# An adaLN, two-way Mamba and FFN kernel: places of side jobs inside its rounds moved by a table

## What is computed

```
h = layernorm(x) * (1 + ca) + sa                       # ca, sa, ga, ...: rows made from a condition vector
for the backward and the forward direction:            # own weights each
    xi, z = split(h @ in_proj.T)                       # 512 channels each
    xi    = silu(causal_conv4(xi) + conv_b)
    dt, B, C = split(xi @ x_proj.T, [64, 80])
    dt    = softplus(dt @ dt_w.T + dt_b)
    state[t] = exp(dt*A) * state[t-1] + (dt*xi)*B[t]   # 16 states for every channel
    y     = sum_s(state * C) + xi*D ;  y = y * silu(z) ; y = sigmoid(y @ out_proj.T)
x = x + ga * (layernorm(0.5*(yf + yb))*g + b + h)
x = x + gb * ffn(layernorm(x) * (1 + cb) + sb)         # four ternary matmuls, silu and gelu
```

## Time and profile before

| | |
|---|---|
| median of 3 runs | 4754.95 us (4752.24 to 4763.35) |
| span of the profiled execution | 4760.7 us |
| DVE busy | 3894.2 us, 82% |
| PE busy | 4479.5 us, 94% |
| POOL busy | 3320.9 us, 70% |
| ACT busy | 3109.7 us, 65% |
| rounds 1 to 30 | 182.6 to 3318.5 us, 101 to 110 us each |

### The profile page before, as it was taken

One profiled execution on the slowest core, in us unless ns is written; L12 is line 12 of the kernel. 1 busy time (PEld: TensorE's weight loads), 2 busy tenths in 40 slices (PEclk: granted clock), 3 DMA queues, 4 the chain that ended last, 5 costly groups with the idle time before them and its releaser, 6 DMA issues. The chain is left out here.

```text
span 4760.7 us, 67108 instructions
## 1 busy us (share of the span) xinstructions
PE 4479.5 (94%) x24932; PEld 3395.1 (71%) x24932; DVE 3894.2 (82%) x4126; ACT 3109.7 (65%) x5158; POOL 3320.9 (70%) x1559
## 2 busy tenths in 40 slices
PE   7999999999999989999999999998799999999999
PEld 3666666666666666667666667666688888888888
DVE  5999999999999999999999999999854444444452
ACT  6777777777777777777777777777444444444443
POOL 4999999999999999999999999999820000000000
PEclk9999999999999999999999999999999999999999
DMA  7544444444444444444444444444231111010100
GB/s 271 178 142 141 134 151 132 136 134 134 143 139 134 155 132 138 129 139 139 131 147 140 129 130 136 143 142 156 103 123 32 36 32 36 32 36 32 36 23 10
DMA packets 297736, 545.76 MB, mean 115 GB/s; under 512 B 101888, under 2 KB 186624, under 8 KB 262784
## 3 DMA queue, kind: packets, MB, share of 16 engines
q1 hardware_dynamic: 296512, 529.91, 35.6%
q10 hardware_dynamic: 896, 11.54, 0.7%
HBM read 502.77 MB, written 50.14 MB: 116 GB/s over the span
## 5 line engine op out<-in xcount | busy, mean ns | idle before, releaser
L1400 DVE TENSOR_TENSOR_SCAN m_h<-bank,m_state,m_dBx 128x512 f32<-128x512 f32 x1512 | 1841.2, 1265 | 35.0 <-ACT bank L1145 27.2
L868 PEld LDWEIGHTS bank<-ident,m_h 128*128 128x128 f32 x8192 | 980.9, 143 | 417.2 <-issue 345.8
L868 PE MATMUL bank<-ident,m_h 128*128 128x128 f32 x8192 | 1197.6, 276 | 12.9 <-DVE m_h L1408 12.8
L1283 POOL TENSOR_TENSOR m_dBx<-u,m_Bs 128x1024 f32<-128x1024 f32 x432 | 1016.4, 2377 | 0.4 <-DMA m_Bs<-b_dram 0.2
L1283 POOL TENSOR_TENSOR m_dBx<-m_u,m_Bs 128x1024 f32<-128x1024 f32 x432 | 1015.5, 2371 | 1.2 <-DMA m_Bs<-b_dram 1.0
L1294 POOL TENSOR_TENSOR m_h<-m_h,m_Cs 128x1024 f32<-128x1024 f32 x384 | 909.4, 2368 | 105.8 <-ACT m_state L1077 105.1
L1408 DVE TENSOR_TENSOR m_h<-m_h,bank 128x1024 f32<-128x1024 f32 x640 | 767.0, 1198 | 51.7 <-PE bank L850 51.4
L1145 ACT ACTIVATE bank<-m_dt,cols 128x512 f32<-128x512 f32 x864 | 584.8, 688 | 225.2 <-DVE m_h L1400 223.7
L1145 ACT ACTIVATE bank<-dt,cols 128x512 f32<-128x512 f32 x864 | 584.1, 688 | 193.6 <-DVE m_h L1400 191.6
L302 POOL TENSOR_TENSOR mvj<-mvj,norm_c 128x4 f32<-128x4 f32 x16 | 16.5, 1032 | 969.0 <-DVE mvj L263 969.0
L731 PE MATMUL bank<-hT,w_in 128*128 128x512 f32 x1024 | 547.4, 630 | 113.1 <-ACT hT L998 105.8
(11 more groups left out here) (177 smaller groups left out, 5847.1 us busy)
## 6 DMA issues: line engine op xcount, KB each, us to landing
m_Bs<-b_dram SPq DMA_DIRECT2D x256, 1024.0 KB, 6.3
m_Cs<-c_dram SPq DMA_DIRECT2D x384, 256.0 KB, 3.7
m_dg<-d_dram SPq DMA_DIRECT2D x160, 256.0 KB, 3.9
xx<-in_x SPq DMA_DIRECT2D x16, 512.0 KB, 4.9
xn_dram<-xx SPq DMA_DIRECT2D x16, 512.0 KB, 4.5
yb_dram<-m_ysb SPq DMA_DIRECT2D x16, 512.0 KB, 5.0
xx<-xn_dram SPq DMA_DIRECT2D x16, 512.0 KB, 3.8
x_dram<-m_ysb SPq DMA_DIRECT2D x16, 512.0 KB, 5.0
```

The costliest lines, as they stand in the source:

```text
L868: mm = pe.matmul(YB[b][:, o:o + P], h[:, k % NH, m, tok:tok + P], ident[:, :], start=(s == 0 and o == 0), stop=False, is_transpose=True, s ...
L1283: pool.tensor_tensor(dBx[:, dbx_ring(ch, k) % NDBX, :, :], u[ch.batch][:, m, :], Bs[:, k // BP % 2, k % BP, :].unsqueeze(1).broadcast_to(( ...
L1400: dve.tensor_tensor_scan(o, decays, share, initial, ALU.mult, ALU.add).then_inc(S["scan"], 1)
```

## The change

Only places change, no operation. The table `AT`, the banks of three jobs, and these constants are new; SP's loads are listed in another order; `job` and `row_job` count the rows of the last round at their new places among the jobs of their bank.

```diff
-AT = {J_LN: (0, 2), J_X: (1, 3, 9, 10), J_CONV: (13, 16, 20, 23), J_DT: (32, 35, 44, 49), J_Z: (51, 52, 56, 58),
-      J_Y: (45, 60, 14, 17), J_OUT: (31, 40), J_UT: (25, 26)}
+AT = {J_LN: (0, 0), J_X: (1, 3, 6, 10), J_CONV: (13, 16, 20, 22), J_DT: (36, 35, 44, 49), J_Z: (50, 53, 56, 58), J_Y: (46, 59, 14, 17), J_OUT: (29, 40), J_UT: (25, 26)}
-AT_B, AT_C = 28, 36
+AT_B, AT_C = 28, 37
-BANK = (0, 1, 0, 1, 0, 1, 0, 1, 0, 1, 1, 1, 1, 0, 1, 0, 1, 0, 1, 1, 0, 1, 0, 0, 0, 0, 0, 0)
+BANK = (0, 1, 0, 0, 0, 1, 0, 1, 0, 1, 1, 1, 1, 0, 1, 0, 1, 0, 1, 0, 0, 1, 0, 0, 1, 0, 0, 0)
-AT_ROWS = (16, 21, 26, 30, 32, 37, 41)
+AT_ROWS = (12, 17, 23, 31, 35, 47, 53)
-P_UNITS = (2, 3, 5, 9, 13, 15, 16, 19, 20, 22, 23, 27)
+P_UNITS = (2, 8, 9, 13, 15, 16, 19, 20, 22, 23, 26, 31)
-EVAC = (44, 12)
-AT_XI, AT_ZS = (24, 31), (24, 31)
-AT_XN = 17
-AT_EXP = (51, 56)
-AT_LNP = (51, 58)
+EVAC = (45, 12)
+AT_XI, AT_ZS = (23, 32), (23, 32)
+AT_XN = 20
+AT_EXP = (51, 59)
+AT_LNP = (54, 59)
-AT_XD = (13, 16, 18, 21)
-ADD_S = (29, 0)
-U_S = (30, 10)
+AT_XD = (13, 16, 19, 22)
+ADD_S = (28, 0)
+U_S = (30, 8)
@@ SP, body: a C load goes behind the load of x, the store of y and of the diagonals ahead of the last C loads
                 load_c(ch, 0)
-                load_c(ch, 1)
                 load_d(ch, 0)
                 load_d(ch, 1)
                 if has(ch, 2):
                     load_x(ch.go(2))
                 if not has(ch, 1):
                     load_ffn(ch)
+                load_c(ch, 1)
                 load_b(ch, 2)
...
                 load_c(ch, 9)
+                if has(ch, -1):
+                    store_y(ch.go(-1))
                 load_d(ch, 3)
                 load_b(ch, 7)
                 load_c(ch, 10)
-                if has(ch, -1):
-                    store_y(ch.go(-1))
+                if has(ch, 1):
+                    store_diagonals(ch.go(1))
                 load_c(ch, 11)
                 load_d(ch, 4)
@@ POOL, flush
-                pool.wait_ge(drain[R_BANK], row_job(len(AT_ROWS)))
+                pool.wait_ge(drain[R_BANK], row_job(len(AT_ROWS) - 1) + 1)
```

More of the change, by code:

```diff
@@ L432, in job @@
                 return b, before(FRONT, FIRST_START)
-            more = len(AT_ROWS) if b == R_BANK and (body == NALL or body == NALL - 1 and i in MID) else 0
+            more = 0
+            if b == R_BANK and body is not None:
+                more = len(AT_ROWS) if body == NALL else sum(a < START[i] for a in AT_ROWS) if body == NALL - 1 else 0
             off = nf - nt + before(MID) + before(TAIL) + before(FRONT)
@@ L443, in row_job, with count @@
         def row_job(e):
-            last = Chunk(NPASS - 1, NC - 1, 1)
-            return job(last, next(i for i in MID if BANK[i] == R_BANK))[1] - len(AT_ROWS) + e
+            def count(jobs, end=STEPS):
+                return sum(BANK[k] == R_BANK and START[k] <= end for k in jobs)
+            nf, nm, nt = count(FRONT), count(MID), count(TAIL)
+            return Chunk(NPASS - 1, NC - 1, 1).at(nf + nm + nt, nf - nt + e) + count(MID, AT_ROWS[e]) + count(TAIL, AT_ROWS[e])
         def wait_filled(eng, ch, i):
@@ L685, in body @@
                 load_c(ch, 3)
+                load_b(ch, 4)
                 load_c(ch, 4)
[L687 to L690, removed]
                 if norms(ch, 2):
                     store_xn(ch.go(2))
+                load_b(ch, 5)
+                load_c(ch, 5)
+                load_c(ch, 6)
+                load_b(ch, 6)
                 load_c(ch, 7)
-                load_b(ch, 6)
+                load_d(ch, 2)
                 if has(ch, 1):
                     store_b(ch.go(1))
-                load_d(ch, 2)
                 load_c(ch, 8)
                 load_c(ch, 9)
+                if has(ch, -1):
+                    store_y(ch.go(-1))
                 load_d(ch, 3)
@@ L707, in body @@
                 if has(ch, 1):
-                    store_diagonals(ch.go(1))
                     load_b(ch.go(1), 0)
+                if has(ch, 1):
                     load_b(ch.go(1), 1)
```

## The result

The changed kernel is slower: 4809.2 us (4801.3 to 4819.7) against 4758.1 us (4752.2 to 4763.4) before, ratio 1.0102, 95% interval 1.0089 to 1.0114. The forecast was 4729.5 us and its range ended at 4757. The slowdown is small, 1%, but its interval is clear of 1.

The account below looks back on a forecast made before the run. DVE bounds the Mamba rounds, so they can win only its 79 us of waits. Terms -30 - 2 - 3 + 2 - 5 + 12.6 = -25.4 us took 4754.95 to 4729.5 us, range 4710 to 4757.

Parts of the forecast that it names:

- SP's new list: SyncE's loads: C and B tiles asked for one or two POOL products later, each with over 3 us left; nil.
- (b): DVE's wait after unit 22 for PE's spread, all 30 rounds, 13.8 us; forecast -3 us, bounds 0 and -13.8.
- Norm and input products: Second transpose to step 0; of DVE's 32.3 us waiting after unit 2 for PE's spread, 30 won, bounds 10 and 32.
- Units exchanged: Units 27, 31, 26, 3, 5, 8 exchanged between POOL and DVE, sums unchanged; cost nil.
- Third input product at step 6: On PE, moved from step 9 into idle time before unit 4, making up for two earlier spreads; nil.
- SiLUs at 23 and 32: DVE's waits behind ACT's two SiLU groups, 33.0 us in 30 rounds; forecast -2 us, bounds -10 and +15.
- First rounds and round 15: Prologue's dt product later; POOL's diagonals and earlier product meet in round 15; +2 us, 0 to 4.
- Rows of the last round: DVE waits 6.3 us there; rows at 35, 47 and 53 stand by themselves; -5 us, bounds -1 and -6.3.
- The end: Unit 31's product ahead of `Gains` on POOL makes the last sum late for DVE's join; +12.6 us, bounds 9 and 14.
- half of (a): Rival: half of DVE's waits after unit 2 for PE's spread stay, slow clock striking other rounds; 4745 us, chance 0.16.
- rival of unit 12: PE loaded more in steps 28 to 33, unit 12's spread late; one slow window a round, 4773 us; chance 0.14.
- a wait of DVE for the product of POOL: Sign that the forecast is wrong: DVE waits for `m_dBx`, meaning POOL is the bound.

Follow-up runs that it names:

- front jobs alone: Kernel before with only the norm's two transposes at step 0, third input product at step 6 and second on bank 0: 4724.4 us, 0.9916.
- mended kernel: Changed kernel, new units kept, SyncE's list ending C tile 10, diagonal tile 4, stores, next round's B tile 0, C tile 11: 4743.1 us, 0.9959.
- the ones with the old units: Changed kernel with the GpSimd units of before and its second small product back at step 10: new SyncE list 0.9918, old list 0.9907.

## Why the prediction was wrong

The step that failed is this one: "SP's new list asks for C and B tiles one or two POOL products later; by the list each still has over 3 us ... Nil." I counted gates in the list, and only for some of the tiles. I gave no time to the stores that SyncE issues between them, though a move costs everything that is passed: 7 us of issue ahead of the diagonal tile and C tile 11, and some more until a tile behind them lands. With the old units the same list costs nothing (0.9996), since in round 5 of that run the stores start 3.4 us before step 50; the exchange of units put their gate one POOL product, 4.7 us, later, so that they start 1.3 us after it. The diagonal tile I never looked at. In the changed kernel this costs 4809.2 against 4743.1, or 1.0102 against 0.9959, 1.4% or 68 us; the waits that it makes, 38 us at steps 62 and 63 and 29.5 us at step 2, come to the same.

The rest by its steps. With the list mended the kernel stands at 0.9959, which is 4735 us on the prediction's median of 4754.95: inside its range, 6 us above its number. That this is so close is partly luck: the exp waits fell by 8 us where 2 were forecast, step 2 waits 11 us more where nothing was, and (b) hardly moved.

- *Norm and input products, 30 us won of 32.3:* right, 31 us by the front jobs alone. The shape was as told where no tile is late: in round 6 of the mended kernel PE waits 1.55 us for DVE's product and 0.31 us for the norm, in the changed one 0.81 and 1.66 us. The spread came in time in both.
- *Units exchanged, nil:* POOL's own products held for the most part (in the mended kernel step 2 still waits, 12.9 us in 15 rounds, where it was 1.6 us before; forecast was nothing), but the gates above were missed.
- *Third input product at step 6, nil:* not tested apart from the norm; together they gave more than the 30 us, 8.4 us less waiting for ACT.
- *SiLUs at 23 and 32, -2:* the exp waits fell from 33.0 to 26.8 us, but the front jobs alone, with the SiLUs at their old places, have 24.6. So no run shows a gain from the move itself.
- *(b), -3 from the y copy and spread at step 45:* hardly anything with the new units, 14.0 us in 31 rounds where it was 14.5; with the old units 12.0, which is about the gain that was forecast, but not in the changed kernel.
- *First rounds and round 15, +2:* round 0 and the prologue +2.2, round 15 +4.9 (109.9 to 114.8). In the mended kernel round 15 takes 111.7, so 1.8 of it belongs to this step and the rest to the late tiles.
- *Rows of the last round, -5:* the last round is 6.0 us shorter in the changed kernel, but 3.5 us of that come with the front jobs alone (104.0), and rows put in beside these gave nothing. Right in sum, for another reason than given; how the remainder is shared between rows and other jobs was not tried.
- *The end, +12.6:* right. From ACT's last copy to the end of POOL's last sum it was 7.4 us (3433.43 - 3426.01) and is now 21.4 (3475.66 - 3454.25), 14.0 more where 13.7 were forecast, and DVE's join waits 13.35 us. By its size it is also most of what parts the mended kernel (0.9959) from the ones with the old units (0.9918 and 0.9907).

Two sums in the prediction do not come out, though neither is why it failed. The chances add up to 0.54 + 0.16 + 0.08 = 0.78, not 0.71. And the high end of 4757 is more than what is named for it: a third of the rival of unit 12 gives 4744, half of (a) with the end at its worst 4746; only both together come to about 4760.

The rival on the slow side was a late spread for unit 12; that spread came in time, and the true rival, a late tile, was not among them. One sign of it was named, a wait of DVE for the product of POOL; it appears as "issue" here, since the product ends just as the scan begins. The other, DVE's wait at steps 62 and 63 for a bank that PE fills with a late diagonal tile, was not named. The rival in which half of (a) stays, because the slow clock strikes other rounds and not fewer, did not come either: TensorE's granted clock was at its lower level (0.50) in 26 stretches of rounds 1 to 30 before, 109 us in all, and in 7 stretches, 27 us, after.

## What to carry to other kernels

Where a queue issues transfers in order and each waits for a buffer, a change of who uses the buffers moves the gates of everything behind them: write out, for each transfer, what it waits for, what is issued ahead of it and how long that takes, and when it is wanted. Slow issues (here four small stores, 7 us) belong behind whatever is wanted next and ahead of whatever has time. A list that is right for one set of users can be far off for another: the same list went from 4764 to 5076 us when one line of units changed. And test the parts of a many-part change alone: here the front jobs alone (0.9916) gave nearly all of the best time measured (0.9907), the exchanged units held the loss, and the others were worth little.

## What the runs showed of the hardware

A store of 2.5 KB takes SyncE as long as several large loads. The view of DMA issues of the kernel before (count, KB each, median us from issue to landing), and the same view of the kernel after:

```profile
m_Bs<-b_dram SPq DMA_DIRECT2D x256, 1024.0 KB, 6.3
m_Cs<-c_dram SPq DMA_DIRECT2D x384, 256.0 KB, 3.7
m_dg<-d_dram SPq DMA_DIRECT2D x160, 256.0 KB, 3.9
...
d_dram<-m_dbB SPq DMA_DIRECT2D x128, 2.5 KB
```

```profile
m_Bs<-b_dram SPq DMA_DIRECT2D x256, 1024.0 KB, 7.3
m_Cs<-c_dram SPq DMA_DIRECT2D x384, 256.0 KB, 4.5
m_dg<-d_dram SPq DMA_DIRECT2D x160, 256.0 KB, 5.6
```

Four such stores, 10 KB in all, took 5.5 to 9.4 us to issue in the rounds shown or named above, where a load of 256 KB ahead of them takes 0.3 to 0.6. A load behind them is slow three times: it is issued later, its own issue takes longer (1.69 us for the C tile at 701.47, 0.32 for the one ahead of the stores), and it takes longer to land. The medians in these views can't show the last, since they run over all tiles and only one C tile in 12 and one diagonal tile in five moved; the two moved tiles do. Medians from issue to landing over rounds 1 to 30: C tile 11 3.5 us ahead of the stores (kernel before), 9.4 us behind them (changed kernel), 9.1 us in the kernel before with only this move; diagonal tile 4 3.9, 7.5 and 7.2 us. One move alone does it, so it is the place behind the stores that makes the landing slow.

The Trainium skill, page "DMA: Bandwidth & Descriptors", Queues, rings and completion order, says that on each DMA engine the descriptors of a queue are consumed in ring order. These traces are in line with that, since in round 5 of the kernel before with the one move the C tile right behind the stores, with nothing issued between, landed 10.0 us after its issue, where it took 3.4 us ahead of them; the order on the single DMA engines is not seen here. How these us divide between the issue, the transfer of the stores and other traffic was not taken apart.
